# Perceiver layer on one core: a reordered opening, drain and ending, the key product from fp32r parts, and the mask converted in place in two buffers

## What is computed

```python
x = x + xattn(layernorm(x), ctx, ctx, mask, gamma, beta)    # softmax over 1601 context rows, then a layernorm
x = x + attn(layernorm(x), W_qkv, W_out)                    # softmax over the 64 tokens of a batch
x = x + ffn(layernorm(x), router_w, expert_w1, expert_w2)   # the best 2 of 8 experts, 512 -> 2048 -> 512, gelu
# in xattn:
logits = einsum('bsd,btd->bst', q, k) / sqrt(d_k)
logits = where(mask == 0, NEG, logits)
```

## Time and profile before

| | us |
|---|---|
| median of 3 runs | 768.18 (767.44 to 768.25) |
| profiled run | 767.6 |
| its span | 765.9 |
| TensorE busy | 736.6 (96%) |
| VectorE busy | 443.4 (58%) |
| ScalarE busy | 309.5 (40%) |
| GpSimd busy | 153.9 (20%) |

### The profile page before, as it was taken

How to read it: one execution, slowest core, us unless ns; L and a number is a source line. 1 busy time by engine, 2 the same in 40 slices (tenths; PEclk the granted TensorE clock), 3 DMA queues, 4 the chain that set the end, 5 groups by cost and what they waited for, 6 DMA issues and landing times.

```text
span 765.9 us, 12386 instructions
## 1 busy us (share of the span) xinstructions
PE 736.6 (96%) x4794; PEld 560.5 (73%) x4794; DVE 443.4 (58%) x1005; ACT 309.5 (40%) x518; POOL 153.9 (20%) x162
## 2 busy tenths in 40 slices
PE   6999999999999999999999999999999999999992
PEld 5444455454545554578999999999998998888882
DVE  5243467676767664886775545555556556555620
ACT  2022212121223221335555555565555666666620
POOL 2132130404132200132310210310211230120201
PEclk9999999999999999999999999999999999999997
DMA  9999999999999999921545545655657565665302
GB/s 328 408 419 418 398 402 418 397 419 402 418 403 417 400 416 398 330 63 32 202 165 196 143 151 194 160 193 179 185 192 199 198 227 193 214 207 216 86 1 28
DMA packets 36333, 199.40 MB, mean 260 GB/s; under 512 B 4700, under 2 KB 5100, under 8 KB 15536
## 3 DMA queue, kind: packets, MB, share of 16 engines
q1 hardware_dynamic: 29912, 186.74, 63.2%
q0 software_dynamic: 4704, 9.14, 6.4%
q10 hardware_dynamic: 1656, 2.70, 1.0%
HBM read 188.19 MB, written 10.37 MB: 259 GB/s over the span
## 4 chain that ended last, share of the span: by engine, by line
PE 82%; DVE 11%; issue 2%; ACT 2%; DMA 1%; POOL 0%; DVEq 0%; POOLq 0%; ACTq 0%
PE ps L805 11%; PE ps L1066 8%; PE ps L1068 8%; PE ps L1067 8%; PE ps L846 7%; PE ps L1088 4%; PE ps L1089 4%; PE ps L1090 4%; PE ps L1095 4%; PE ps L1096 4%; PE ps L1097 4%; PE ps L773 4%; DVE xn_parts L1432 2%; PE ps L826 2%; PE ps L780 1%
## 5 line engine op out<-in xcount | busy, mean ns | idle before, releaser
L479 POOL TENSOR_TENSOR small<-small 128x1 f32<-128x1 f32 x64 | 24.1, 377 | 556.3 <-DVE yb_space L1669 197.4
L1068 PE MATMUL ps<-xT,low_a 128*128 128x288 f32 (+5 forms) x384 | 110.1, 287 | 0.0
L1274 ACT ACTIVATE hid<-ps 128x288 f32<-128x288 f32 (+5 forms) x128 | 50.6, 396 | 143.7 <-PE ps L1068 141.1
L1638 DVE TENSOR_TENSOR h_ring<-hid,h_ring 128x288 fp32r<-128x288 f32 (+5 forms) x128 | 55.7, 436 | 86.1 <-ACT h_ring L1279 86.0
L1501 DVE TENSOR_TENSOR low_a<-w_raw_a,high_b 128x2048 fp32r<-128x2048 f32 x32 | 73.4, 2292 | 39.2 <-ACT high_b L1202 39.2
L846 PE MATMUL ps<-arena 128*64 128x512 f32 (+1 forms) x416 | 94.1, 597 | 0.8 <-DVE arena L1401 0.8
L805 PE MATMUL ps<-arena 128*64 128x512 f32 x384 | 85.5, 596 | 0.2 <-ACT arena L1149 0.2
L1142 ACT COPY arena<-ps 128x512 f32<-128x512 f32 (+2 forms) x89 | 41.4, 525 | 100.6 <-PE ps L780 61.3
L1066 PE MATMUL ps<-xT,high_b 128*128 128x288 f32 (+5 forms) x256 | 74.9, 292 | 0.0
L1067 PE MATMUL ps<-xT,high_b 128*128 128x288 f32 (+5 forms) x256 | 73.4, 287 | 0.0
L1068 PEld LDWEIGHTS ps<-xT,low_a 128*128 128x128 f32 x384 | 72.4, 189 | 0.0
(11 more groups left out here) (217 smaller groups left out, 1644.7 us busy)
## 6 DMA issues: line engine op xcount, KB each, us to landing
arena<-in_ctx_turned SPq DMA_DIRECT2D x48, 1024.0 KB, 20.4
arena<-in_ctx SPq DMA_DIRECT2D x48, 1024.0 KB, 18.7
w_raw_a<-in_w SPq DMA_DIRECT2D x48, 1024.0 KB, 4.8
w_raw_b<-in_w SPq DMA_DIRECT2D x16, 1024.0 KB, 4.8
arena<-in_mask SPq DMA_DIRECT2D x8, 800.5 KB, 22.1
tokens_x<-arena SPq DMA_DIRECT2D x11, 256.0 KB, 12.4
arena<-in_w_qkv SPq DMA_DIRECT2D x8, 256.0 KB, 4.8
out<-res SPq DMA_DIRECT2D x8, 256.0 KB, 9.2
```

The source lines that it names most:

```text
L1068: mm = pe.matmul(o, w_low[2 * f][:, cols], high[:, k, 0:w.width], start=False, stop=(k == KC - 1))
L1274: nc.scalar.activation(hid[:, c % 2, 0:w.width], bank(c % UP_BANKS)[:, 0:w.width], ACT.Gelu).then_inc(gelu_done, 1)
L1638: dve.tensor_tensor(h_ring[:, c % RING, 1, 0:w.width], hid[:, c % 2, 0:w.width], h_ring[:, c % RING, 0, 0:w.width].bitcast(F32), ALU.subtr ...
```

## The change

1. Opening. The identity has a load of its own, ahead of the other constants; 6 warm-up transposes; the fold of the key matrix waits for one turned block at a time; the values weights are turned between the second and the third score block of tile 0, and the query and rest of tile 1 come before the second fold.
2. The key matrix is kept as an fp32r high part (ScalarE) and low part (VectorE). `keys` runs 32 products with the high part of the rows and, behind a wait for the low part, 16 with the low part. The high part of the rows is rounded straight from PSUM, before the fp32 copy.
3. Mask, bound and probabilities share one buffer a tile, in two buffers. The mask of tile `r+1` is loaded at the head of round `r`, once the probabilities of tile `r-1` are turned, and converted after the sending of tile `r-3`. `low_xn` runs between the two masking operations.
4. Drain. Another order on all engines: values of tile 7 split round its own scores, both `hot_rows` behind the last `ranks`, gates and second routing steps behind the hot places, and weight splits 1 and 2 later.
5. Start of the experts. The order of the experts is computed in chunk 1; splits 2, 3, 4 in chunks 0 and 2.
6. Ending. The last three `down` of the last window run for its first tile and then for its second.

```diff
-    for kind in ("xq", "rest0", "rest1", "qr"):
+    for kind in ("xq", "rest0", "rest1"):
         yield kind, 0, 0
-    for which in ("wv", "vo"):
-        for n in range(KC):
-            yield which, 0, n
+    for n in range(KC):
+        yield "wv", 0, n
+    yield "qr", 0, 0
     for kind in ("xq", "rest0", "rest1"):
         yield kind, 1, 0
+    for n in range(KC):
+        yield "vo", 0, n
...
-        mask_sb = arena[:, 8192:8192 + T].bitcast(I32)
-        bound = arena[:, 9793:9793 + T]
-        prob = arena[:, 11394:11394 + T]
+        prob = [arena[:, 8192 + i * T:8192 + (i + 1) * T] for i in range(2)]
...
             def load_mask(p):
-                if p >= 1:
-                    sp.wait_ge(bound_ready, p)
-                sp.dma_start(mask_sb, mask[p * P:(p + 1) * P, :]).then_inc(mask_in, 16)
+                if p >= 2:
+                    sp.wait_ge(filled, filled_at("p", p - 2, NBLK - 1))
+                sp.dma_start(prob[p % 2].bitcast(I32), mask[p * P:(p + 1) * P, :]).then_inc(mask_in[p % 2], 16)
...
             for r in range(1, TILES):
                 if runs(r + 1):
+                    load_mask(r + 1)
                     for blk in range(NBLK - 1):
                         load_turned(r + 1, blk)
...
                 for blk in range(NBLK - 1):
                     load_ctx(r, blk)
-                    if blk == 0 and runs(r + 2):
-                        load_mask(r + 2)
...
                 add_bias(r)
+                if runs(r - 3):
+                    send(r - 3)
                 if runs(r + 1):
                     bounds(r + 1)
-                if runs(r - 3):
-                    send(r - 3)
...
             def keys(t):
 
-                wait_copied(pe, "xn", t)
+                pe.wait_ge(xn_high, t + 1)
                 o = open_fill("g", t)
                 for hc in range(KC):
+                    cols = slice(hc * P, (hc + 1) * P)
                     for k in range(KC):
-                        mm = pe.matmul(o[:, hc * P:(hc + 1) * P], scores_w[:, k, hc * P:(hc + 1) * P], xnT[:, k, :],
-                                       start=(k == 0), stop=(k == KC - 1))
+                        pe.matmul(o[:, cols], scores_high[:, k, cols], xn_parts[:, 0, k, :],
+                                  start=(hc == k == 0), stop=False)
+                        pe.matmul(o[:, cols], scores_low[k][:, cols], xn_parts[:, 0, k, :], start=False, stop=False)
+                pe.wait_ge(xn_split, t + 1)
+                for hc in range(KC):
+                    cols = slice(hc * P, (hc + 1) * P)
+                    for k in range(KC):
+                        mm = pe.matmul(o[:, cols], scores_high[:, k, cols], xn_parts[:, 1, k, :],
+                                       start=False, stop=(hc == k == KC - 1))
                 mm.then_inc(filled, 1)
...
-            pe.wait_ge(cst_in, 16)
-            keep_busy(16, bank(0))
+            pe.wait_ge(id_in, 16)
+            keep_busy(6, bank(0))
...
-            for blk in range(NBLK - 1):
-                scores(0, blk)
-            rest_scores(0)
+            scores(0, 0)
+            scores(0, 1)
             pe.wait_ge(wv_in, 16)
             for hc in range(KC):
                 turn_weights("wv", raw_v, hc)
+            scores(0, 2)
+            rest_scores(0)
+            turn_query(1)
+            turn_rest(1)
             pe.wait_ge(wo_in, 16)
...
             keys(LAST)
+            values(LAST, range(1))
+            own_scores(LAST)
+            values(LAST, range(1, KC - 1))
+            turn_own_probs(LAST)
+            values(LAST, range(KC - 1, KC))
             turn_second(LAST - 1)
-            own_scores(LAST)
+            weigh(LAST)
             router(LAST - 1)
-            values(LAST)
-            turn_own_probs(LAST)
-            ranks(LAST - 1)
-            weigh(LAST)
             first_rows()
-            hot_rows(LAST - 1)
             turn_second(LAST)
             keep_busy(4, open_fill("logit", LAST))
             router(LAST)
-            keep_busy(18, open_fill("rank", LAST))
+            ranks(LAST - 1)
+            keep_busy(20, open_fill("rank", LAST))
             ranks(LAST)
+            hot_rows(LAST - 1)
             hot_rows(LAST)
...
                     up(w, c)
-                    if c >= LAG:
+                    if w.kind == EXPERTS - 1 and c == FC - 1:
+                        for t in range(2):
+                            for late in range(FC - 1 - LAG, FC):
+                                down(w, late, t)
+                    elif c >= LAG:
                         down(w, c - LAG)
...
-                wait_copied(act, "xn", t)
+                act.wait_ge(filled, filled_at("xn", t))
                 if t >= 1:
                     act.wait_ge(filled, filled_at("u", t - 1))
-                act.copy(xn_parts[:, 0, :, :], xnT).then_inc(xn_high, 1)
+                act.copy(xn_parts[:, 0, :, :], by_chunk(bank(bank_at("xn", t)))).then_inc(xn_high, 1)
...
+                    if blk == 1 and runs(j - 2):
+                        low_xn(j - 2)
...
             route_first(LAST - 2)
-            for j in range(2):
-                split_low(STATIC[0], j)
+            split_low(STATIC[0], 0)
+            low_xn(LAST - 1)
...
+            second_norm(LAST)
             route_first(LAST - 1)
-            copy_pt(LAST)
+            route_first(LAST)
+            hot_places(LAST - 1)
+            hot_places(LAST)
+            route_second(LAST - 1)
+            route_second(LAST)
             gates(LAST - 1)
...
+            gates(LAST)
+            split_low(STATIC[0], 1)
...
                     low_h(w, c)
+                    if w.kind == 0 and c == 0:
+                        split_low(w, 2)
                     if w.kind == 0 and c == 1:
+                        count_order()
+                    if w.kind == 0 and c == 2:
                         split_low(w, 3)
+                        split_low(w, 4)
...
-                    if (due := block_due(w.kind, c)):
+                    if (due := block_due(w.kind, c)) and (w.kind or c):
                         split_low(STATIC[due[0]], due[1])
```

More of the change, by code:

```diff
@@ L104, in by_act @@
 def by_act(kind, t, n):
-    if kind == "xn":
-        return t != LAST
-    return n % 2 == 0 if kind in ("wq", "wk", "m") else kind not in ("vo", "out", "qr", "logit", "rank", "pt")
+    if kind == "pt":
+        return t == LAST - 1
+    return n % 2 == 0 if kind in ("wq", "wk") else kind not in ("m", "vo", "out", "qr", "logit", "rank")
 ACTS = [by_act(kind, t, n) for kind, t, n in FILLS]
@@ L345, in build @@
         w_low = [low_a[:, j, :] for j in range(6)] + [low_b[:, j, :] for j in range(2)]
-        w_high = ([high_a[:, j, :] for j in range(2)] + [high_b[:, j, :] for j in range(4)]
+        w_high = ([high_a[:, 0, :], high_b[:, 0, :], high_a[:, 1, :]] + [high_b[:, j, :] for j in range(1, 4)]
                   + [high_c[:, j, :] for j in range(2)])
@@ L386, in build @@
         used = rt(1).bitcast(I32)
-        hot_place = rt(1)
+        hot_place = [rt(1) for _ in range(2)]
         more_e, more_at = rt(MORE).bitcast(I32), rt(MORE).bitcast(I32)
@@ L405, in build @@
         rest_here = [sem(f"rest_here{i}") for i in range(RESTS)]
-        mask_in = sem("mask_in")
+        mask_in = [sem(f"mask_in{i}") for i in range(2)]
         v_own, p_own = sem("v_own"), sem("p_own")
@@ L872, in own_scores, with values @@
                 mm.then_inc(filled, 1)
-            def values(t):
-                pe.wait_ge(xn_split, t + 1)
+            def values(t, rows=range(KC)):
                 o = open_fill("u", t)
-                for k in range(KC):
+                for k in rows:
                     high, low = xn_parts[:, 0, k, :], xn_parts[:, 1, k, :]
@@ L1069, in up, with down @@
                 mm.then_inc(up_done, 1)
-            def down(w, c):
+            def down(w, c, only=None):
                 f, q = divmod(c, 4)
@@ L1093, in down @@
                     for t, (a, m) in enumerate(w.tiles):
+                        if only is not None and t != only:
+                            continue
                         o = bank(y_bank(w, t))[0:m, :]
@@ L1119, in _ @@
                     more = in_use(pe)
-            for c in range(FC - LAG, FC):
-                down(STATIC[-1], c)
             with pe.If(more > 0):
@@ L1213, in _ @@
             act.dma_start(rw_sb, w_router.rearrange("p (k e) -> p k e", k=KC)).then_inc(rw_in, 16)
-            for n in range(0, KC, 2):
-                copy_fill("m", 0, scores_w[:, n, :], n)
+            for n in range(KC):
+                act.wait_ge(filled, filled_at("m", 0, n))
+                act.copy(scores_high[:, n, :], bank(bank_at("m", 0, n))).then_inc(m_high, 1)
             copy_query(0)
@@ L1384, in softmax @@
                 wait_copied(dve, "qr", j)
-                own.then_next(dve.tensor_reduce(top, prob, AX.X, ALU.max))
+                own.then_next(dve.tensor_reduce(top, row, AX.X, ALU.max))
```

(12 more changed lines are left out.)

144 lines of the change are left out of this document (70 added, 74 removed).

## The result

The changed kernel takes 775.99 us (774.91 to 776.73, 4 runs) where the kernel before takes 768.21 beside it (767.44 to 768.88, 4 runs): a ratio of 1.0101 with a 95% interval of 1.0086 to 1.0117, slower by 7.8 us. Four more runs in a later series gave 776.25 us (774.18 to 777.46) and 1.0116 (1.0094 to 1.0138). The profiled execution took 776.64 us with a span of 775.0, 9.1 us more than the span of before.

A forecast was written before the change was run, and what follows sets the result against it. Rounds bound by TensorE's own instructions, transfers next, VectorE's chain third. Terms 9.9 - 2.7 + 1.0 - 1.9 + 0.3 + 1.7 - 1.3 = +7.0 us on the median 768.18 gave 775.2 us, own range 771.5 to 779.0.

The forecast's parts named there:

- Key product: Keys in TensorE-bound rounds 2 to 7: 48 fp32r products at 0.111 us, +1.65 us a tile, +9.9 us.
- the idle start: First product after an idle stretch takes 0.34 us, the next 0.23; so the fp32r weight load is 0.11 us.
- the streaming end: Lower bound of the key product's pace: 0.063 us at 128 columns, 3.0 us a tile, -0.65.
- rival (a): Key product: fp32r weights of 128 columns load in the time of streaming or less; 759 us, chance 0.10.
- Own-probability waits: TensorE's waits before the own probabilities' transpose go: 1.48 us once, 0.3 in four other rounds; -2.7 us.
- Held norm of round 2: Mask conversion of tile 3 holds VectorE's second normalisation in round 2, TensorE's transpose comes late; +1.0 us once.
- Opening: TensorE reaches its scores some 3 us earlier, but not all of it stays; -1.9 us (-2.5 to -0.5).
- Drain: New orders behind the rounds: +0.3 us with the clock held, about +2 without; the first taken.
- Start of the experts: TensorE waits for VectorE's splits, gates and order of experts before the fourth hidden chunk; +1.7 us (0 to 3).
- Ending: Last three down products run tile by tile, so the second scatter starts earlier; -1.3 us (-1.6 to 0).
- (b): Keys as forecast, but the old waits stay and the clock falls again in the drain; 779.6 us, chance 0.13.
- (c): No wait at the experts' start, and the opening keeps all of its 2.5 us; 772.9 us, chance 0.15.

The follow-up runs named there:

- the run with halved products: Changed kernel, part of computation left out: even tiles with 64 moving columns in the key product, odd tiles with 64 weight columns; 886.39 us.
- the one with the halves: Changed kernel with GpSimd's conversion of a mask as two operations (1024 and 577 columns), the second behind the first; 775.73 us in a single run.
- the run with the three edits: Changed kernel with fp32 keys, the mask's conversion in two operations, one weight split of the first expert later; 763.14 us, ratio 0.9944 to the kernel before.

## Why the prediction was right, point by point

The forecast was 775.2 us, measured 775.99. The sum of the terms was +7.0 us; the spans differ by 9.1, the medians by 7.8. Part of the 2 us is luck of the profiled execution, part are terms off in size: by term the misses are +0.5, -0.35, +0.17, +0.6, +1.25, -0.35 and +0.1 us. That the median came within 0.8 us is thus partly luck; the mechanism of each term but the drain is what the traces show.

- **Key product.** +9.9 forecast, +10.4 measured, 1.74 us a tile and not 1.65. The pace was right; the small rest is the hand-over at both ends, which I took off the old product (3.75 us from start to start, for which I put 3.7) and never added to the new one: 48 x 0.111 is 5.33, and the product takes 5.48. The step from the idle start to "the load is 0.11 us in fp32r too" is borne out by the run with halved products. A pace near the streaming end, 0.063 us, appears once the weights are 64 columns wide. One of my two points for that end was misread: the 0.112 us of the products with 240 columns is the same 0.11 us as with 8, 64 and 128 moving columns, so it was the load and not the streaming, and it told for fp32r already what I took from the idle start. So rival (a) is out: the rule of the Trainium skill (TensorE: Matmul & The Clock Gate, section on weight-path perf modes) that loads of 128 weights of a type other than FP32 are fast does not cover fp32r as used here.
- **Own-probability waits.** -2.7 forecast, -3.05 measured. The excess is some 0.2 us in round 3, where I took the marked wait of 1.48 though the transpose came 1.88 us behind the product before it and the pace is 0.23, and 0.1 us in round 2 (0.41 for 0.3). That the cause is not VectorE's order is now shown by a run; that it is GpSimd's conversion rests on the rows and on elimination.
- **Held norm of round 2.** +1.0 forecast, +1.17 measured. The mask landed at 113.6 us (estimate: 113) and VectorE's operation was held to 117.9.
- **Opening.** -1.9 forecast, -1.30 measured. The round-1 scores started at 57.96 (57.8 forecast); the rest was lost at the third score block of round 2, whose transfer landed at 91.64 us and not at 91.1. How much is kept changes by execution: in eleven traces the same opening started that block between 91.01 and 92.91 us, which makes the term anything from -2.0 to -0.1; the two latest are those whose clock fell in the opening, for which my range (-2.5 to -0.5) had nothing. I put -1.9 though my own estimate of that landing left 92.98 - 91.1 = 1.88 at most.
- **Drain.** +0.3 forecast, +1.55 in this execution. The step that failed is "I take the first, since 20 warm-up transposes stand right before". The clock fell at 355.0 us, ahead of these 20 and not behind them, and the transposes, at half clock, held back ranks whose operands VectorE had finished at 357.4 us, until 359.16. Of the four profiled executions with these instructions two lost the clock here (this one and the one with the halves) and two kept it; in those two the term is -0.05 us (some 1.6 less), beside an execution of before whose clock did fall. Held or fallen, my two prices (+0.3, +2) were each within 0.5 us; the choice between them was wrong, since the same program does both.
- **Start of the experts.** +1.7 forecast, +1.35 measured, with the wait where I put it (1.08 us at the fourth down product). My sum of VectorE's operations was 0.35 us too long.
- **Ending.** -1.3 forecast, -1.19 measured.
- **Rivals (b) and (c).** (b) was half right: the old waits did not stay, the fall of the clock did. (c), with no wait at the experts' start, did not occur.

What makes the changed kernel slower is thus one term, the keys: 10.4 us in the rounds, and more inside the drain. With them in fp32 the kernel is level with the one before (1.0037, 0.9998 to 1.0076) and not 3.6 us ahead of it as I expected; in the profiled execution two longer stretches at half clock, 1.4 us each, account for the difference.

## What to carry to other kernels

Count TensorE instructions with 128 moving columns by their weight loads: splitting one fp32 product (two instructions) into three fp32r ones makes three loads of two, 0.34 us for 0.23, and the cheaper streaming is never seen. With 512 moving columns it pays: the first fold of the kernel before takes 0.43 us an instruction (32 from 14.31 to 28.12), 0.86 us a product, and three fp32r products take 0.70. Before an operation is shortened or moved, find who holds it: here a long GpSimd operation on SBUF held VectorE's operations that were issued in it, and moving or cutting the GpSimd operation was what helped. Cost TensorE's clock at both levels and carry both in the range: in this drain of thin products and short waits, the same program got the one or the other.

## What was not expected of the hardware

- An fp32r product with 128 weight columns takes 0.111 us with 128 or 64 moving columns, and 0.06 us with 64 weight columns. At a granted clock of 0.50 the one with 64 moving columns takes 0.22 us, so the load slows down with the clock.
- In each of the four tiles with 48 products of 64 moving columns the granted clock went from 1.00 to 0.50, 2.4 to 3.9 us into them and for 7 to 10 us; with 128 moving columns it never did in the six rounds of the changed kernel. The profile shows TensorE as busy throughout in both.
- A wait of 2.7 us in the middle of full work was followed by 0.50 for 3.5 us, in both executions that had it; waits of 0.8 to 1.3 us in the same stretch were not, in the executions profiled, but one of 0.78 us at 301 us was, in one execution of several.
- GpSimd's conversion of 1601 columns held VectorE's next operation with two SBUF sources until 4.14 us into its 5.62 (an operation of 0.22 us took 3.42 in one trace and 1.83 in another, and ended at the same point). The Trainium skill (SBUF — State Buffer, section on the two separate sides) says that the first comer holds the shared ports for the whole instruction. Here the two-source operations got through before the conversion ended. A cast with one source did not: in the kernel before it stood behind the subtraction in four rounds, took 1.05 us for 0.16, and each time ended within 0.04 us of the conversion's end. The rows, of VectorE before, then of GpSimd and VectorE after:

```profile
212.79 1.05 DVE L1472 CAST route<-route 128x2 int32<-128x2 f32 x1
...
113.79 5.62 POOL L622 TENSOR_SCALAR arena<-arena 128x1601 f32<-128x1601 int32 x1
116.09 1.83 DVE L1361 SCALAR_TENSOR_TENSOR small<-small 128x1 f32<-128x1 f32 x1
```

- With 1024 columns the hold of a two-source operation ended at 1.05 us or sooner of 3.64, in the run with the three edits, far less than in proportion. Why is open.
